# A graph layer whose edge sort ends in two parts: the first 128 columns and 64 of its 832 gathers ahead of the rest

## The reference

```
xn = layernorm(x); feats = xn @ W (4 heads of 64)
z = s_self[src] + s_neigh[dst]; e = leaky(z) * edge_weight
alpha = softmax of e over the edges of each src node
out[src] += alpha * feats[dst]
x = x + relu(out + bias) + linear_attention(xn); x = x + experts(layernorm(x))
```

## Time and profile before

| | us |
|---|---|
| median of 3 runs | 2411.05 |
| lowest and highest of them | 2404.05, 2411.13 |
| the profiled execution | 2398.86 |
| its span, first to last instruction | 2397.1 |
| first stage, to the last swap | about 531 |
| gathers of the stream, first and last start | 546.4, 1613.9 |

### The profile page before, as it was taken

The page is one execution under the profiler, slowest core; times in us unless marked ns, Lnnn a source line. Parts: engine busy times, 40 slices in busy tenths (PEclk is TensorE's granted clock), DMA queues, the critical chain, the costliest instruction groups (busy, mean ns, idle before and its releaser), DMA issues. The chain is left out here.

```text
span 2397.1 us, 38652 instructions
## 1 busy us (share of the span) xinstructions
PE 1681.5 (70%) x8046; PEld 1259.4 (53%) x8046; DVE 1756.0 (73%) x4645; ACT 1393.3 (58%) x4627; POOL 1309.4 (55%) x1245
## 2 busy tenths in 40 slices
PE   3899961115676777777767888766641999999965
PEld 2455531012454555555445555533541999999854
DVE  6988899985588888899867777677860555555468
ACT  2555553322687887879786878796430444444344
POOL 2333310006777777777777777770575555555521
PEclk9999985557678777767888989888555999999988
DMA  6333320005456565564746555541970333333354
GB/s 206 132 124 138 135 88 0 0 29 173 141 153 203 165 201 165 165 196 138 221 136 180 151 159 154 163 115 37 259 102 18 104 106 106 103 105 106 95 176 153
DMA packets 167253, 317.72 MB, mean 133 GB/s; under 512 B 34358, under 2 KB 102627, under 8 KB 167089
## 3 DMA queue, kind: packets, MB, share of 16 engines
q1 hardware_dynamic: 104654, 166.68, 20.9%
q0 software_dynamic: 54176, 140.57, 20.7%
q10 hardware_dynamic: 8256, 8.68, 2.0%
HBM read 248.17 MB, written 67.65 MB: 132 GB/s over the span
## 5 line engine op out<-in xcount | busy, mean ns | idle before, releaser
L934 POOL DMA_INDIRECT big<-feat_d,pair_idx x832 | 815.3, 980 | 265.7 <-issue 188.9
L961 ACT ACTIVATE big<-big 128x64 f32<-128x64 f32 x3328 | 800.5, 333 | 0.9
L1057 PE MATMUL wide<-big 128*128 128x260 f32 x1664 | 606.5, 488 | 152.8 <-DVE big L1367 113.7
L1057 PEld LDWEIGHTS wide<-big 128*128 128x128 f32 x1664 | 332.8, 231 | 249.9 <-issue 210.6
L1367 DVE TENSOR_TENSOR big<-big,wide 128x260 f32 x832 | 350.9, 422 | 119.1 <-PE wide L1057 52.5
L1348 DVE TENSOR_TENSOR big<-wide,pair_rel 128x128 f32<-128x128 f32 x832 | 233.6, 282 | 0.0
L296 ACT ACTIVATE big<-big 128x896 f32<-128x896 f32 (+2 forms) x153 | 136.9, 895 | 161.4 <-DVE big L522 147.6
L2051 PEld LDWEIGHTS p_h<-xT,w_sb 128*128 128x128 f32 x1808 | 220.4, 193 | 5.7
L2051 PE MATMUL p_h<-xT,w_sb 128*128 128x128 f32 x1808 | 220.8, 276 | 0.0
L268 POOL TENSOR_SCALAR xn<-X,mean,rstd 128x256 f32<-128x256 f32 x49 | 101.8, 2078 | 210.4 <-PE p_t L600 177.8
L2062 PE MATMUL p_o<-w_sb,hT 128*128 128x256 f32 x904 | 213.9, 379 | 1.1 <-DVE w_sb L2000 1.1
(11 more groups left out here) (329 smaller groups left out, 2675.9 us busy)
## 6 DMA issues: line engine op xcount, KB each, us to landing
big<-code_d SPq DMA_DIRECT2D x52, 512.0 KB
kv_d<-big SPq DMA_DIRECT2D x49, 512.0 KB, 2.6
X<-kv_d SPq DMA_DIRECT2D x12, 2048.0 KB, 13.0
big<-in_L_ffn_w_dram SPq DMA_DIRECT2D x32, 512.0 KB
b_sb<-in_L_ffn_b_dram SPq DMA_DIRECT2D x113, 128.0 KB, 3.0
big<-feat_d,pair_idx POOLq DMA_INDIRECT x832
big<-moe_d SPq DMA_DIRECT2D x7, 1792.0 KB, 9.9
feat_d<-feat_sb SPq DMA_DIRECT2D x49, 130.0 KB, 2.7
```

Of the source, the lines that this page charges most:

```text
L934: nc.gpsimd.indirect_dma_start(out=rows[:, n // SB % RB, n % SB, :], out_offset=None, in_=m["feat_d"], in_offset=bass.IndirectOffsetOnAxis ...
L961: ins = nc.scalar.activation(rows[:, b, s, cols], rows[:, b, s, cols], ACT.Copy, scale=rows[:, b, s, HF + h:HF + h + 1])
L1057: nc.tensor.matmul(sums[s % RING][:, 0:HF + H], onehot[:, s // GP % 2, s % GP, :], rows[:, b, s, :], start=True, stop=True).then_inc(summe ...
```

## The change

The seven last swaps leave the first stage. At the beginning of the second, VectorE does their key part for columns 0 to 127 alone, seven steps of 64 pairs of columns, keeping the seven masks; then it makes a short map, by the same way as the full one, for the first F = 64 pairs, while the weight part of the seven steps goes on in columns 0 to 127 (three before `first_pick`, four after). ScalarE copies the 64 columns into `pair_idx`, and GpSimd begins to gather. Then the seven swaps are done for columns 128 to 895, and the full map follows as before; GpSimd waits for it at the 65th gather. The scratch of the short map lies in columns of `onehot`, in the dead key buffer and in PSUM banks that the full map uses later.

```diff
+    plan, final = plan[:-7], plan[-7:]
+    m["final"] = [(j, at) for _, _, j, at, *_ in final]
...
 gpsimd:
-            pool.wait_ge(pair_copied, 1)
+            pool.wait_ge(f_copied, 1)
             for n in range(PAIRS):
+                if n == F:
+                    pool.wait_ge(pair_copied, 1)
...
 scalar:
+            for n in range(4):
+                copy_lead(n)
+            act.wait_ge(f_idx, 1)
+            nc.scalar.activation(pair_idx[:, 0:F], first_idx, ACT.Copy).then_inc(f_copied, 1)
+            for n in range(4, 7):
+                copy_lead(n)
+            for n, (_, at) in enumerate(m["final"]):
+                if n:
+                    act.wait_ge(rest_weights, n)
+                nc.scalar.activation(m["wgt"][:, 1 - at, P:CH], m["wgt"][:, at, P:CH], ACT.Copy).then_inc(rest_copied, 1)
...
 tensor:
+            pe.wait_ge(f_passes, 1)
+            nc.tensor.matmul(first_chunk, ones_b, first_passes, start=True, stop=True).then_inc(f_chunk, 1)
+            pe.wait_ge(f_code, 1)
+            pe.wait_ge(f_pick, 1)
+            nc.tensor.matmul(first_idx, first_dst, first_pick, start=True, stop=True).then_inc(f_idx, 1)
...
 vector:
+            def swap_keys(bit, at, cols, mk, masked, swapped):
+                nc.vector.tensor_tensor(folded(mk, bit), lo, hi, ALU.is_gt).then_inc(masked, 1)
+                nc.vector.tensor_tensor(to[0], lo, hi, ALU.min)
+                nc.vector.tensor_tensor(to[1], lo, hi, ALU.max).then_inc(swapped, 1)
+            def swap_weights(bit, at, cols, mk, swapped):
+                nc.vector.copy_predicated(...).then_inc(swapped, 1)
+            LEAD, REST = slice(0, P), slice(P, CH)
+            for n, (bit, at) in enumerate(m["final"]):
+                swap_keys(bit, at, LEAD, lead_mask(n), lead_masked, lead_keys)
             (first_row, as before)
+            chain(step_i[:, 0:1]); chain(step_f[:, 0:1], min); chain(step_f[:, 0:1], + place_f)
+            nc.vector.tensor_scalar(first_passes, iota_f[:, 0:F], step_f[:, 0:1], None, ALU.is_gt).then_inc(f_passes, 1)
+            chain(nc.vector.tensor_scalar(first_code[:, 0:P], keys.bitcast(I32)[:, 0:P], 0, LOW, ...))
+            nc.vector.tensor_scalar(first_dst, first_code[:, 0:P], N - 1, None, ALU.min).then_inc(f_code, 1)
+            for n in range(3):
+                lead_swap(n)
+            dve.wait_ge(f_chunk, 1)
+            nc.vector.tensor_scalar(first_pick, first_chunk, place_f[:, 0:1], None, ALU.is_equal).then_inc(f_pick, 1)
+            for n in range(3, 7):
+                lead_swap(n)
+            for n in range(7):
+                rest_swap(n)
             (the full map, as before)
```

More of the change, by code:

```diff
@@ L173, in nodes_and_sort @@
     m["sorted_in"] = buf
+    plan, final = plan[:-7], plan[-7:]
+    assert all(kind == "swap" for kind, *_ in final)
+    m["final"] = [(j, at) for _, _, j, at, *_ in final]
     GROUPS = NT // GT
@@ L765, in edge_stream @@
     last = big[0:1, 4 * CH:4 * CH + PAIRS]
+    F = RB * SB
+    fresh = line[:, CH + PAIRS:]
+    first_dst, first_pick, first_passes = fresh[:, 0:P], fresh[:, P:P + F], fresh[:, P + F:P + F + F // 2].bitcast(BF16)
+    first_chunk, first_idx = wide[2][:, 0:F], wide[2][:, 512:512 + F]
+    first_code = spare_k.bitcast(I32)
+    mask = big[:, 6 * CH + 1024:6 * CH + 1024 + 448]
     place_f, step_f, step_i = sb("place_f", [P, Q]), sb("step_f", [P, Q]), sb("step_i", [P, Q], I32)
@@ L774, in edge_stream @@
     lane_made = sem("lane_made")
+    lead_keys, lead_masked, lead_copied, lead_weights = sem("lead_keys"), sem("lead_masked"), sem("lead_copied"), sem("lead_weights")
+    rest_keys, rest_masked, rest_copied, rest_weights = sem("rest_keys"), sem("rest_masked"), sem("rest_copied"), sem("rest_weights")
+    f_passes, f_chunk, f_code, f_pick, f_idx, f_copied = (
+        sem("first_passes"), sem("first_chunk"), sem("first_code"), sem("first_pick"), sem("first_idx"), sem("first_copied"))
     kv_in, squared, var_made, v_scaled, dots_done = (
@@ L989, in take @@
                 nc.scalar.activation(out, bank, ACT.Copy).then_inc(pair_copied, 1)
-            take(1, pair_idx[:, 0:half], wide[1][:, 0:half])
+            take(1, pair_idx[:, F:half], wide[1][:, F:half])
             take(3, pair_w[:, 0:half], wide[3][:, 0:half])
@@ L1156, in product @@
                 return ins
+            pe.wait_ge(f_copied, 1)
             in_w = weights.rearrange("p (q l) -> p q l", l=P)
@@ L1193, in chain, with halves, folded @@
                 dve.wait_ge(fin.sem, fin.value())
+            def halves(t, bit):
+                v = t.rearrange("p (g two c) -> p g two c", two=2, c=1 << bit)
+                return v[:, :, 0, :], v[:, :, 1, :]
+            def folded(t, bit):
+                return t.rearrange("p (g c) -> p g c", c=1 << bit)
+            def swap_keys(bit, at, cols, mk, masked, swapped):
+                lo, hi = halves(m["key"][:, at, cols], bit)
+                to = halves(m["key"][:, 1 - at, cols], bit)
+                nc.vector.tensor_tensor(folded(mk, bit), lo, hi, ALU.is_gt).then_inc(masked, 1)
+                nc.vector.tensor_tensor(to[0], lo, hi, ALU.min)
+                nc.vector.tensor_tensor(to[1], lo, hi, ALU.max).then_inc(swapped, 1)
@@ new lines, in swap_weights @@
+            def swap_weights(bit, at, cols, mk, swapped):
+                width = cols.stop - cols.start
+                pairs = "p (g two c) -> p g two c"
+                nc.vector.copy_predicated(
+                    m["wgt"][:, 1 - at, cols].rearrange(pairs, two=2, c=1 << bit),
+                    folded(mk, bit).bitcast(U32).unsqueeze(2).to_broadcast([P, width >> (bit + 1), 2, 1 << bit]),
+                    m["wgt"][:, at, cols].rearrange(pairs, two=2, c=1 << bit)[:, :, ::-1, :]).then_inc(swapped, 1)
@@ new lines, in _, with lead_mask, lead_swap, rest_swap @@
+            LEAD, REST = slice(0, P), slice(P, CH)
+            def lead_mask(n):
+                return mask[:, n * P // 2:(n + 1) * P // 2]
+            def lead_swap(n):
+                bit, at = m["final"][n]
+                dve.wait_ge(lead_copied, n + 1)
+                dve.wait_ge(lead_masked, n + 1)
+                if n:
+                    dve.wait_ge(lead_weights, n)
+                swap_weights(bit, at, LEAD, lead_mask(n), lead_weights)
+            def rest_swap(n):
+                bit, at = m["final"][n]
+                if n:
+                    dve.wait_ge(rest_keys, n)
+                    dve.wait_ge(rest_weights, n)
+                else:
+                    dve.wait_ge(lead_weights, 7)
+                swap_keys(bit, at, REST, mask[:, 0:(CH - P) // 2], rest_masked, rest_keys)
+                dve.wait_ge(rest_copied, n + 1)
+                dve.wait_ge(rest_masked, n + 1)
+                swap_weights(bit, at, REST, mask[:, 0:(CH - P) // 2], rest_weights)
@@ L1195, in _ @@
+            for n, (bit, at) in enumerate(m["final"]):
+                if n:
+                    dve.wait_ge(lead_keys, n)
+                swap_keys(bit, at, LEAD, lead_mask(n), lead_masked, lead_keys)
+            dve.wait_ge(lead_keys, 7)
             nc.vector.memset(first_row[:, HF:HF + H], TINY).then_inc(first_made, 1)
@@ L1198, in _ @@
             dve.wait_ge(prep_made, 3)
+            chain(nc.vector.tensor_scalar(step_i[:, 0:1], keys.bitcast(I32)[:, P - 1:P], 20, 63, ALU.logical_shift_right, ALU.bitwise_and))
+            chain(nc.vector.tensor_scalar(step_f[:, 0:1], step_i[:, 0:1], NT - 1, None, ALU.min))
+            chain(nc.vector.tensor_tensor(step_f[:, 0:1], step_f[:, 0:1], place_f[:, 0:1], ALU.add))
+            nc.vector.tensor_scalar(first_passes, iota_f[:, 0:F], step_f[:, 0:1], None, ALU.is_gt).then_inc(f_passes, 1)
+            chain(nc.vector.tensor_scalar(first_code[:, 0:P], keys.bitcast(I32)[:, 0:P], 0, LOW, ALU.logical_shift_right, ALU.bitwise_and))
+            nc.vector.tensor_scalar(first_dst, first_code[:, 0:P], N - 1, None, ALU.min).then_inc(f_code, 1)
[7 more added lines that the diff above has]
+                rest_swap(n)
+            dve.wait_ge(rest_keys, 7)
+            dve.wait_ge(rest_weights, 7)
             chain(nc.vector.tensor_scalar(ahead[:], place_f[:], float(NCH), float(2 * CH), ALU.is_ge, ALU.mult))
```

5 lines of the change are left out of this document (added).

## The result

| | before | after |
|---|---|---|
| first measurement, median (us) | 2410.07 (2404.05 to 2411.13, 4 runs) | 2374.94 (2373.55 to 2382.04, 4 runs) |
| ratio, 95% interval | | 0.9874 [0.9842, 0.9905] |
| measured again, in other rounds | 2403.05 (2396.85 to 2408.29, 23 runs) | 2382.54 (2372.76 to 2387.46, 6 runs) |
| ratio, 95% interval | | 0.9916 [0.9896, 0.9936] |

The changed kernel is faster, by 35 us in the first measurement and by 20.5 in the second; 15.7 were forecast. The profiled execution of the changed kernel took 2382.04, 16.8 less than that of before.

What follows compares the result with a forecast made beforehand. The GpSimd gather train, running without a break, was taken to bound the stage's end. A 24.9 us earlier start less 6.6 and 2.6 lost gives 15.7: 2383.2 profiled, 2395 as median; range 2385 to 2407, likeliest case 2392 to 2401.

Steps and rivals of the forecast that it cites:

- The lead: Start of second stage to first gather: short map ready at about 521.5, so the first gather comes 24.9 us earlier.
- the ring: Places for gathers ahead of VectorE's additions: 12.7 us of room at the 65th gather, so no hold was forecast.
- the size of the loss at the head: Gathers beside late swaps lose 6.6 us (4.0 to 8.4), beside the map's making 2.6 (1.5 to 4).
- the middle: Gathers under the late swaps: 2.04 us each, taken between 1.63 and 2.45; 8.4 gathers in 17.15 us, not 13.7.
- the map's making: 10.8 us of VectorE work on the full map: 1.79 us a gather, 2.6 us lost (1.5 to 4).
- the base: Time the gain is taken from: profiled execution 2398.86, 12.2 below the runs' median 2411.05; the same step gives 2395.
- The range: Whole kernel: from 2385, swaps not touching gathers with the runs' spread of 3.5, to 2407, gathers standing still.
- a rival: Late swaps: the claim that they don't touch the gathers, 2389; gathers of up to 2.96 spoke against it; chance 0.14.
- the swaps don't touch the gathers: Rival on the late swaps: only the map's making costs, 22.3 us gained, 2389; chance 0.14.
- they stand still: Rival on the late swaps: no gather is let in under them, 5.2 us gained, 2406; chance 0.12.
- the slower case: Rival: no gathers let in under swaps or map's making, train starts where the map leaves VectorE, 2416; chance 0.05.
- The late front: Rival at the stream's front: map slips 17.5 us or more, ring holds the train; at 25, 2403; chance 0.07.

Runs made afterwards that it cites:

- The pair with the head products in PSUM: Before and changed kernel, each with rkv, the later v scaling's factor, moved to PSUM: 2389.18 us (0.9948) and 2367.60 us (0.9856 of before).
- the experiment that did hold them: Changed kernel with rkv in PSUM, first gather made to wait until the last rest swap is done: 2382.09 us, 0.9928, against 2366.71 without the wait.
- The further edits at the head: Changed kernel with rkv and late swaps' masks in PSUM: 2367.36 us, 0.9872; with a shorter way to the first gather too: 2368.21 us, 0.9860.

## Why the prediction failed

**The lead held.** First gather 24.5 us earlier by the end of the first stage (24.9 forecast), key swaps at 0.53 (0.5), the bias all but free, the map's first instruction 5.6 later (4.75; a rest swap takes 2.52 in place of 2.45). VectorE paid that from its waits for blocks 0 and 1, which are both gone (some 5 had been forecast to stay at block 1), and the ring didn't hold the 65th gather.

**The step that failed is the size of the loss at the head.** The working had the right reading beside the wrong one: let in at the next boundary, 1.63 each; let in once a swap, 2.45; "I take the middle, 2.04". Measured: 1.62. The two rows at hand both showed a gather let in at the end of its operation. Only the longest gathers last past the end of a second operation, and the first trace of before has six of over 2.5 us among 832. The evidence stood near one end, and the middle gave the other as much weight. So with the map's making: 1.79 came from the four gathers that stood beside such work, taken as the rule for all; 1.42 was measured. So 5.2 us were lost in place of 9.2, and 24.5 - 5.2 gives 19.3 at the 65th gather. The pair with the head products in PSUM, where the spread is small, says 19.6 there and 21.6 in the times, of which up to 2.6 may be the two waits of before.

**The second step is the base.** The forecast carried the step from the median of three runs, 2411.05, and took the rest of the train to keep its pace. It doesn't: in the traces of the two kernels gathers 65 to 448 took 12.1 to 21.1 us more than 0.946 each, and 4.5 to 5.6 with `rkv` in PSUM. With before's median of 23 runs, 2403.05, and the 19.3 of the 65th gather the sum is 2383.8, against 2382.54 measured then. Of the 20.4 us between the forecast (2395.35 unrounded) and the first result, 8.0 are this base, 7.6 the changed kernel's own low draw (2374.94 against 2382.54), and 4.0 the loss at the head. The range had 3.5 us for this spread, at its lower end alone. That a gather may take up to 2.96 us stood in the earlier trace rows and was used against a rival; what those gathers cost in all was not asked.

**The rivals.** That the swaps don't touch the gathers is wrong by the spacing of 1.62 and right by none of its steps, though its time lay nearer. That they stand still, and the slower case, fell with the experiment that did hold them. The late front did not come; but the ring's limit that it spoke of is real. With the head products in PSUM it holds the changed kernel's train once the head gains 4 us more, and it holds two gathers of the kernel before, whose head is late.

The Trainium skill, "SBUF — State Buffer", section "Who interferes with whom", says that a VectorE instruction with at most one SBUF input doesn't contend with GpSimd, outside of the faster modes. The runs agree: one input moved to PSUM, and 24 gathers that meet a scaling are 0.02 us longer in all. The same section of the Trainium skill says that a `tensor_tensor` did not stall DMA issue in its probe; these gathers, whose indices lie in SBUF, were held for up to 2 us (2.96 in place of 0.95) beside the scaling, which is one.

What stays open: what decides in an execution how many gathers meet a scaling, and why the first measurement drew before high and after low at once. That these meetings make up that draw is an inference from the spread that goes with them; those executions have no traces but the two shown. The changed kernel's two traces fit it (2382.04 with 14.7 us of meetings, 2372.76 with 8.9). Before's two don't: the slower one (2405.92) has 14.9 and the faster one (2398.86) 18.4, and there the late first gather weighs more.

The best version is the changed kernel with the head products in PSUM, 0.9856 and 0.9869 of before in two measurements. The further edits at the head are level with it.

## What to carry to other kernels

Where a rate has two readings, price each by the rows that show it, and don't take the middle with one that no row shows. Before the gain of an edit is weighed in parts per thousand, ask what makes the executions differ: here the long tail of one instruction's line (0.946 in the median, 2.96 at most) was worth 12 to 15 us, more than half of what the change brought. Here a GpSimd queue that sets the end of a stage was slowed by VectorE instructions beside it with two SBUF inputs; look for a small operand that can move to PSUM, first in the work that has nothing to do with the queue. A train that starts before the map also no longer waits for products whose time hangs on the granted clock.

## What the runs showed of the hardware

- A gather that starts inside a VectorE instruction with two SBUF inputs ends some 0.8 us after that instruction (529.80 after 528.98, 531.62 after 530.83). One that such an instruction reaches 0.32 after its start (939.90, 940.22) was not done in the 0.47 us between that one and the next, and ended 0.83 after the next, at 942.86, 2.96 long.
- For an exchange with its mask in PSUM the gather isn't held: that of 530.46, 0.94 long, starts inside the exchange of 530.19 and ends 0.21 after it.
- An instruction with one bf16 tensor in SBUF and a column (the making of `hot_t`) held a gather too: that of 698.11 was 1.34 long and ended 0.82 after it.
- Two trains on two engines can fall into step, two gathers in 2.51 and a swap in 2.52, and meeting then costs 0.01 to 0.02 a gather.
- With the granted clock at 0.50 from 546 to 551, where another execution had 1.00, the kernel before waited 9.17 us for its map's products in place of 6.32, and its gathers started as much later.
